# A graph network's first node stage: plain transposes, a split behind PSUM, and a longer pipeline

## What is computed

```python
# first layer (src, dst: edges; loops of weight 1 are added for every node)
deg = segment_sum(w_all, dst_all)
norm = deg**-0.5[src_all] * w_all * deg**-0.5[dst_all]
y = relu(segment_sum((x @ W)[src_all] * norm[:, None], dst_all) + b)
x1 = layernorm(x + y)
# second layer: per edge a filter from 20 radial numbers, scalar and vector
# products with the gathered x1[dst], a sum into x1's rows of src, two more
# matmuls, then out = layernorm(x1 + ...)
```

## Time and profile before

| what | us |
|---|---|
| median of 3 runs | 1240.66 |
| lowest and highest run | 1238.07, 1240.92 |
| the profiled execution | 1237.18 |
| its span | 1235.4 |
| PE busy in the span | 1004.6 (81%) |
| DVE, ACT, POOL busy | 840.1, 699.5, 657.0 |
| first and last start of L818 (nodes0) | 367.0, 664.1 |

### The profile page before, as it was taken

How to read it: one execution, slowest core, us unless ns; L and a number is a source line. 1 busy time by engine, 2 the same in 40 slices (tenths; PEclk the granted TensorE clock), 3 DMA queues, 4 the chain that set the end, 5 groups by cost and what they waited for, 6 DMA issues and landing times.

```text
span 1235.4 us, 23211 instructions
## 1 busy us (share of the span) xinstructions
PE 1004.6 (81%) x5088; PEld 788.5 (64%) x5088; DVE 840.1 (68%) x2538; ACT 699.5 (57%) x1632; POOL 657.0 (53%) x812
## 2 busy tenths in 40 slices
PE   6579998988749999999994788888888888834443
PEld 6557776776538888888883566666666666523332
DVE  7588777767327777777774566666566666448887
ACT  0168778867626666666663344343444434358887
POOL 2048888888547777777775455555555554310000
PEclk9999999989859999999998899999999999955555
DMA  9949999999976888888886678787777877579998
GB/s 359 419 147 242 242 253 231 248 236 237 214 177 212 271 283 277 282 279 279 278 276 213 178 176 182 170 171 178 168 173 176 183 168 155 77 204 348 349 350 296
DMA packets 175015, 289.00 MB, mean 234 GB/s; under 512 B 18514, under 2 KB 75750, under 8 KB 174966
## 3 DMA queue, kind: packets, MB, share of 16 engines
q1 hardware_dynamic: 120982, 176.23, 41.9%
q0 software_dynamic: 35840, 83.91, 36.0%
q10 hardware_dynamic: 18144, 28.32, 6.1%
HBM read 139.49 MB, written 148.90 MB: 233 GB/s over the span
## 4 chain that ended last, share of the span: by engine, by line
PE 28%; issue 18%; POOL 11%; DMA 5%; DVE 4%; ACT 4%; POOLq 2%; SPq 2%; DVEq 0%; ACTq 0%
PE bank L1079 6%; PE bank L1090 4%; PE bank L1100 4%; POOL tiny L463 3%; DMA node_mem<-sum 3%; PE bank L1088 3%; PE bank L1102 3%; PE bank L1103 3%; POOL tiny L466 3%; PE bank L1072 2%; PE bank L1086 1%; PE bank L1080 1%; POOL G_lo L476 1%; POOL tiny L470 1%; POOL tiny L468 1%
## 5 line engine op out<-in xcount | busy, mean ns | idle before, releaser
L500 POOL DMA_INDIRECT sum<-R_mem,l_sidx x80 | 127.9, 1599 | 173.7 <-ACT R_mem L636 167.4
L449 POOL DMA_INDIRECT sum<-R_mem,sidx_all x80 | 131.1, 1639 | 51.1 <-issue 29.3
L1052 PE MATMUL bank<-W0h,G_hi 128*128 128x512 f32 x320 | 134.0, 419 | 0.9 <-ACT G_lo L600 0.9
L1052 PE MATMUL bank<-W0h,G_lo 128*128 128x512 f32 x320 | 126.6, 396 | 0.0
L1052 PE MATMUL bank<-W0l,G_hi 128*128 128x512 f32 x320 | 126.3, 395 | 0.0
L611 ACT ACTIVATE node_mem<-node_mem,tiny 128x512 f32<-128x512 f32 x80 | 65.4, 817 | 91.2 <-POOL tiny L472 91.2
L476 POOL TENSOR_TENSOR G_lo<-node_mem,G_hi 128x512 fp32r<-128x512 f32 x80 | 104.1, 1301 | 19.4 <-ACT G_hi L607 19.4
L875 DVE SCALAR_TENSOR_TENSOR edge_mem<-edge_mem,Y,bank 128x128 f32<-128x128 f32 x240 | 73.1, 388 | 57.2 <-ACT edge_mem L630 42.5
L630 ACT COPY edge_mem<-bank 128x256 f32<-128x256 f32 x80 | 29.8, 372 | 135.8 <-PE bank L1090 135.8
L979 PE MATMUL bank<-G_hi,M_mem 128*128 128x512 f32 x200 | 88.4, 442 | 17.3 <-ACT R_mem L544 15.7
L492 POOL DMA_INDIRECT G_mem<-x_d,dst_i x80 | 79.5, 993 | 35.4 <-issue 16.2
(11 more groups left out here) (172 smaller groups left out, 2995.7 us busy)
## 6 DMA issues: line engine op xcount, KB each, us to landing
sum<-zeros ACTq DMA_DIRECT2D x42, 512.0 KB
filt_d<-node_mem SPq DMA_DIRECT2D x40, 512.0 KB
node_mem<-sum SPq DMA_DIRECT2D x80, 256.0 KB, 2.7
G_mem<-x SPq DMA_DIRECT2D x80, 256.0 KB, 2.8
x_d<-node_mem SPq DMA_DIRECT2D x80, 256.0 KB, 2.1
node_mem<-filt_d SPq DMA_DIRECT2D x80, 256.0 KB
sum<-node_mem SPq DMA_DIRECT2D x80, 192.0 KB, 2.3
out<-G_mem SPq DMA_DIRECT2D x20, 512.0 KB, 4.2
```

The costliest lines, as they stand in the source:

```text
L449: pool.indirect_dma_start(sum0, bass.IndirectOffsetOnAxis(ap=sidx[:, t:t + 1], axis=0), R[t % 8][:, :], None, compute_op=ALU.add).then_inc ...
L500: pool.indirect_dma_start(sum1, bass.IndirectOffsetOnAxis(ap=l1_sidx[:, t:t + 1], axis=0), R3[t % 8][:, :], None, compute_op=ALU.add).then ...
L1052: ins = pe.matmul(bank[4 + a][:, :], zt[b][:, c * P:(c + 1) * P], w[:, c, :], start=(c == 0 and k == 0), stop=(c == 3 and k == 2))
```

## The change

In nodes0:
- The identity of type f32r goes. PE transposes z itself (f32, four plain transposes), in step t + 1, into one of four banks.
- The split moves behind PSUM: ACT copies the bank to zT_hi (f32r) in step t + 2, DVE subtracts zT_hi from the bank into zT_lo in the same step. Each has four buffers. z_hi and z_lo, with ACT's L607, POOL's L476 and ACT's L600, go.
- PE runs the eight products with zT_hi first, then waits for zT_lo and runs the other four.
- DVE's max and sum (L827) go: ACT does Relu in place, POOL adds x, both in step t + 4. bn_stats and bn_aggr come two steps after that, in step t + 6. DVE's bank * dis + b stands last in its step.
- Ln, Exp and the root are done for two tiles at once, in every second step, on ACT and POOL; the root has seven instructions instead of five for one tile. The normalisation comes in step t + 9.
- res has eight buffers instead of four. SP stores in step t + 12, and its loads of sl wait for the transposes, its loads of xl for POOL's sum.
- Lead and tail of the loops grow (DVE, ACT and POOL: lead 16, tail 6 or 9; SP: lead 16, tail 12).

In edges0 the twelve gather semaphores become three, one for each group of four, and ACT waits once per group.

```diff
 @@ SP nodes0
-                    held(sp_, n_hi, s - 3)
-                    held(sp_, n_lo, s - 3)
+                    held(sp_, n_tr, s - 3)
                     sp_.dma_start(sl[a], rows(sum0, s)).then_inc(n_sl[a], 16)
-                    held(sp_, n_res, K_RES * (s - 7))
+                    held(sp_, n_sum, s - 7)
                     sp_.dma_start(xl[u], rows(x, s)).then_inc(n_xl[u], 16)
-                if live(s, 8):
-                    t = s - 8
+                if live(s, 12):
+                    t, a = s - 12, (u - 12) % 8
                     held(sp_, n_x1, t + 1)
...
 @@ POOL nodes0
+                if live(s, 7) and u % 2 == 0:
+                    t, a = s - 8, u // 2
+                    w, mean, var = tiny[a], mv[a][:, :, 0], mv[a][:, :, 1]
+                    st = Stage(n_rstd, g, K_ROOT)
+                    held(pool, n_mv, t + 2)
+                    st.mark(pool.tensor_scalar(w[:, 0, :], var, EPS, None, ALU.add))
+                    st.mark(pool.tensor_scalar(w[:, 7, :], mean, -1.0, None, ALU.mult))
+                    held(pool, n_rs, 2 * (g + 1))
+                    st.mark(pool.tensor_tensor(w[:, 3, :], w[:, 2, :], w[:, 2, :], ALU.mult))
+                    st.settle(pool)
+                    st.mark(pool.tensor_tensor(w[:, 4, :], w[:, 3, :], w[:, 0, :], ALU.mult))
                     held(pool, n_rstd, st.reached())
+                    st.mark(pool.tensor_scalar(w[:, 3, :], w[:, 4, :], -0.5, 1.5, ALU.mult, ALU.add))
                     st.settle(pool)
+                    st.mark(pool.tensor_tensor(w[:, 5, :], w[:, 3, :], w[:, 2, :], ALU.mult))
+                    st.settle(pool)
+                    st.mark(pool.tensor_tensor(w[:, 6, :], w[:, 7, :], w[:, 5, :], ALU.mult))
-                if live(s, 0):
-                    pool.wait_ge(n_hi, s + 1)
-                    wait(pool, n_tr, s - 3)
-                    pool.tensor_tensor(z_lo[u][:, :], sl[u], z_hi[u][:, :].bitcast(F32), ALU.subtract).then_inc(n_lo, 1)
+                if live(s, 4):
+                    t, a = s - 4, (u - 4) % 8
+                    pool.wait_ge(n_rel, t + 1)
+                    pool.tensor_tensor(res[a], res[a], xl[a], ALU.add).then_inc(n_sum, 1)
...
 @@ ACT edges0
+                    act.wait_ge(e_gather[(s - 1) % (NG // 4)], 64 * ((s - 1) // (NG // 4) + 1))
                     for q in (3, 2, 1, 0):
                         t = 4 * (s - 1) + q
-                        act.wait_ge(e_gather[t % NG], 16 * (t // NG + 1))
...
 @@ ACT nodes0, new order of a step
+                if tail:
+                    act.wait_ge(n_mv, t + 2)
+                    act.activation(tiny[a][:, 1, :], mv[a][:, :, 1], ACT.Ln, bias=eps_c[:, :]).then_inc(n_rs, 1)
                 if live(s, 2):
+                    t2, b = s - 2, (u - 2) % 4
+                    act.wait_ge(n_tr, t2 + 1)
+                    wait(act, n_mm, t2 - 3)
+                    act.copy(zT_hi[b][:, :], bank[b][:, :]).then_inc(n_hi, 1)
                     act.dma_start(sum1[bass.ds(t2 * P, P), 0:C], zeros[:, 0:C]).then_inc(s_zero1, 16)
+                if tail:
+                    act.wait_ge(n_rs, 2 * g + 1)
+                    act.activation(tiny[a][:, 2, :], tiny[a][:, 1, :], ACT.Exp, scale=-0.5).then_inc(n_rs, 1)
+                if live(s, 4):
+                    act.wait_ge(n_pre, t4 + 1)
+                    act.activation(res[c], res[c], ACT.Relu).then_inc(n_rel, 1)
+                if live(s, 9):
+                    act.wait_ge(n_rstd, K_ROOT * (g8 + 1))
+                    act.activation(res[c], res[c], ACT.Identity, bias=tiny[b][:, 6, k:k + 1], scale=tiny[b][:, 5, k:k + 1]) \
                        .then_inc(n_x1, 1)
...
 @@ DVE nodes0, new order of a step (z of step s, unchanged, stands first)
+                if live(s, 6):
+                    dve.wait_ge(n_sum, t + 1)
+                    dve.bn_stats(stat[c][:, :], res[a]).then_inc(n_bn, 1)
+                if live(s, 2):
+                    t, b = s - 2, (u - 2) % 4
+                    dve.wait_ge(n_hi, t + 1)
+                    wait(dve, n_mm, t - 3)
+                    dve.tensor_tensor(zT_lo[b][:, :], bank[b][:, :], zT_hi[b][:, :].bitcast(F32), ALU.subtract).then_inc(n_lo, 1)
+                if live(s, 6):
+                    if k == 0:
+                        held(dve, n_x1, t - 6)
+                    held(dve, n_bn, t + 1)
+                    dve.bn_aggr(mv[b][:, k, :], stat[a % 4][:, :]).then_inc(n_mv, 1)
                 if live(s, 4):
+                    dve.wait_ge(n_mm, t + 1)
+                    wait(dve, n_st[a], 32 * turn(t, a, 8))
+                    dve.scalar_tensor_tensor(res[a], bank[4 + c][:, :], dis[:, bass.ds(t, 1)], b0_s[:, :],
+                                             ALU.mult, ALU.add).then_inc(n_pre, 1)
...
 @@ PE nodes0
+                if live(s, 1):
+                    pe.wait_ge(n_z, t + 1)
+                    wait(pe, n_lo, t - 3)
+                    for c in range(4):
+                        ins = pe.transpose(bank[a][:, c * P:(c + 1) * P], sl[a][:, c * P:(c + 1) * P], ident[:, :])
+                    ins.then_inc(n_tr, 1)
                 if live(s, 3):
                     pe.wait_ge(n_hi, t + 1)
+                    wait(pe, n_pre, t - 3)
                     for c in range(4):
+                        for w in (W0h, W0l):
+                            pe.matmul(bank[4 + a][:, :], zT_hi[a][:, c * P:(c + 1) * P], w[:, c, :],
+                                      start=(c == 0 and w is W0h), stop=False)
+                    pe.wait_ge(n_lo, t + 1)
+                    for c in range(4):
+                        ins = pe.matmul(bank[4 + a][:, :], zT_lo[a][:, c * P:(c + 1) * P], W0h[:, c, :],
+                                        start=False, stop=(c == 3))
                     ins.then_inc(n_mm, 1)
```

More of the change, by code:

```diff
@@ L186, in build @@
         G_hi, G_lo = (ring(name, 8, [P, D], F32R) for name in ("G_hi", "G_lo"))
-        z_hi, z_lo = G_hi[:4], G_lo[:4]
+        zT_hi, zT_lo = G_hi[:4], G_lo[:4]
         NG = 12
@@ L190, in build @@
         junk1 = [b[:, 3 * D:3 * D + 256] for b in node_mem]
-        sl, res, W0_s = ([b[:, q * D:(q + 1) * D] for b in node_mem] for q in range(3))
+        sl, W0_s = ([b[:, q * D:(q + 1) * D] for b in node_mem] for q in (0, 2))
+        res = [b[:, q * D:(q + 1) * D] for q in (1, 2) for b in node_mem]
         xl = G
-        zT_hi, zT_lo = G_hi[4:6], G_lo[4:6]
         stat = ring("stat", 4, [P, 6])
-        mv = ring("mv", 4, [P, 2])
-        tiny = ring("tiny", 4, [P, 8])
+        mv = ring("mv", 4, [P, 2, 2])
+        tiny = ring("tiny", 4, [P, 8, 2])
         wst = [b[:, 0:1024].rearrange("p (v d) -> p v d", v=2) for b in node_mem]
@@ L247, in build @@
         e_lo = sem("e_lo")
-        e_gather = [sem(f"e_gather{i}") for i in range(NG)]
+        e_gather = [sem(f"e_gather{i}") for i in range(NG // 4)]
         e_M = sem("e_M")
@@ L267, in build @@
         n_x1 = sem("n_x1")
-        n_st = [sem(f"n_st{i}") for i in range(4)]
+        n_st = [sem(f"n_st{i}") for i in range(8)]
         f_trow = [sem(f"f_trow{i}") for i in range(4)]
@@ L586, in nodes0 @@
             def nodes0(s, u):
-                if live(s, 5):
-                    t, a = s - 5, (u - 5) % 4
-                    act.wait_ge(n_res, K_RES * (t + 1))
-                    act.activation(tiny[a][:, 1:2], mv[a][:, 1:2], ACT.Ln, bias=eps_c[:, :]).then_inc(n_rs, 1)
-                if live(s, 2):
-                    b, t2 = u % 2, s - 2
-                    act.wait_ge(n_tr, s - 1)
-                    wait(act, n_mm, s - 3)
-                    act.copy(zT_hi[b][:, :], bank[b][:, :]).then_inc(n_zT, 1)
@@ L608, in nodes0 @@
[L608 to L611 removed]
+                tail = live(s, 7) and u % 2 == 0
+                if tail:
+                    t, a = s - 8, u // 2
+                    g = t // 2 if isinstance(t, int) else (t - u) // 2 + a
+                    act.wait_ge(n_mv, t + 2)
+                    act.activation(tiny[a][:, 1, :], mv[a][:, :, 1], ACT.Ln, bias=eps_c[:, :]).then_inc(n_rs, 1)
@@ L1044, in nodes0 @@
                     ins.then_inc(n_tr, 1)
                 if live(s, 3):
-                    t, a, b = s - 3, (u - 3) % 4, (u - 3) % 2
-                    pe.wait_ge(n_zT, 2 * (t + 1))
-                    wait(pe, n_res, K_RES * (t - 3))
+                    t, a = s - 3, (u - 3) % 4
+                    pe.wait_ge(n_hi, t + 1)
+                    wait(pe, n_pre, t - 3)
                     for c in range(4):
-                        for k, (zt, w) in enumerate(((zT_hi, W0h), (zT_hi, W0l), (zT_lo, W0h))):
-                            ins = pe.matmul(bank[4 + a][:, :], zt[b][:, c * P:(c + 1) * P], w[:, c, :],
-                                            start=(c == 0 and k == 0), stop=(c == 3 and k == 2))
+                        for w in (W0h, W0l):
+                            pe.matmul(bank[4 + a][:, :], zT_hi[a][:, c * P:(c + 1) * P], w[:, c, :],
```

(1 more changed line is left out.)

94 lines of the change are left out of this document (27 added, 67 removed).

## The result

The changed kernel takes 1207.3 us (median of 4 runs, 1205.0 to 1213.0), the kernel before 1240.3 us: ratio 0.9744, 95% interval 0.9708 to 0.9780. That is 33 us less by the medians. The profiled executions took 1207.2 and 1237.2 us, so 30.0 us less, where the sum of the prediction gave 14.4 less.

The account below looks back on a forecast made before the run. The prediction took POOL's chain, 3.76 us per tile, as the bound, replaced by a 3.51 us DVE-ACT loop. With 1 us of head and 17.1 of drain the stage lost 14.4 us: 1224.5 us forecast, range 1206 to 1242.

Parts of the forecast that it names:

- the release to DVE: Loop term from the end of ACT's zT_hi to the begin of DVE's zT_lo: 0.14 us, read at L630 and L875.
- the drain: End of nodes0 after tile 77: POOL does three sums and three roots in a row, 17.1 us with normalisations.
- the head: Start of nodes0: with fewer transposes the clock may rise later, so the stage's first steps come 1 us later.
- POOL's own chain: Nodes0 in the kernel before: POOL's instructions set 3.76 us per tile, with PE 0.1 us behind.
- The loop that takes over: One-step loop in nodes0, DVE's bank x dis + bias, ACT's Relu to zT_hi, DVE's zT_lo and bn_aggr: 3.51 us.
- the lower end: Low end of the DVE-ACT loop: 3.36 us if releases cost 0.03 each and Relu is as short as the copy.
- two anchors: Whole kernel: 1222.8 us from the profiled execution and 1226.3 from the median of runs; 1224.5 taken between.
- the parts that I costed at nothing: Loads stay hidden, SP's longer lag lies under this, merged gather semaphores and dropping ident_r count for nothing.
- The weighed rule: Next DVE operation waits until the pipe is empty: loop 3.68 us, about 1238 us; part of the no-change rival, chance 0.11.
- The clock: Rival: PE idles 0.34 us per step, clock falls to 1.2 GHz, stage over 200 us longer; chance 0.02.
- PE as the bound: Rival in nodes0: loop terms overlap more than read, PE's 3.17 us per tile bounds, about 1198 us; chance 0.12.
- The slow case: Rival: Relu and neighbours run end to end, loop 3.96 us, about 1259 us, decides from 3.70; chance 0.15 including clock.

Follow-up runs that it names:

- experiment 6: Kernel before with only Ln, Exp and root done for two tiles at once, eight res buffers, later normalisation and stores; 1230.7 us, ratio 0.9913.
- experiment 1: Changed kernel with the normalisation placed ahead of Relu in ACT's step; 1196.0 us, ratio 0.9646.
- experiment 3: Changed kernel with bank x dis + bias moved to the front of DVE's step, ahead of z; 1196.4 us, ratio 0.9639.
- experiment 4: Changed kernel with one more ACT instruction per tile, a Relu of a constant tile, right behind Relu; 1246.1 us, ratio 1.0052.
- experiment 5: Changed kernel with one more ACT instruction per tile, a Relu of a constant tile, ahead of the wait before Relu; 1209.0 us, ratio 0.9745.
- experiment 8: Changed kernel with the DMA of zeros issued by SP instead of ACT; 1210.9 us, ratio 0.9750.
- experiment 9: Changed kernel with SP's stores in step t + 11 instead of t + 12; 1212.3 us, ratio 0.9786.
- experiment 10: Changed kernel with SP's stores in step t + 10 instead of t + 12; 1292.4 us, ratio 1.0428.
- experiment 7: Changed kernel with max and sum again one DVE instruction, one step behind bank x dis + bias, without ACT's Relu and POOL's sum; 1194.0 us, ratio 0.9614.
- experiment 2: Changed kernel with bank x dis + bias moved right behind z, ahead of bn_stats and zT_lo, on DVE; 1208.7 us, ratio 0.9740.

## Why the prediction was right or wrong

In short: the mechanism was right, a loop of one step between DVE and ACT; the sum was wrong in size. It gave 14.4 us less, and the stage became 31.5 us shorter. The terms that were mis-sized are the release to DVE above all, then the drain and the head.

**What bounds the kernel before: right.** POOL's own chain at 3.76 us and PE 0.1 us behind: experiment 6 lightened POOL and got PE's 3.65. The reading missed one thing in that chain: L463 took 0.53 us there because DVE was reading SBUF at that time (see the last section), and 0.21 us alone. Without that, POOL would have needed some 3.4 us (an estimate: 3.76 less 0.32) and not been the bound.

**The loop that takes over: right in kind, too long by 0.13 us per tile.** Both its waits appear in nearly every tile, and experiments 1, 3, 4 and 5 show that it bounds. The forecast had 3.51 us. The step between the L840 of tile 0 (364.60) and of tile 77 (624.77) is 3.38 us, 10.1 us less over 77 tiles. The terms:
- the release to DVE was the step that failed most: 0.14 from the earlier trace rows, measured 0.03 (at the median of 73 releases of L828; none is above 0.04). That is 0.11 x 77 = 8.5 of the 10.1 us. In the earlier trace rows the waiting instruction L875 takes its scalar at an address that depends on the tile, `Y[:, bass.ds(t, 1), i]`, which in the hardware loop comes from a register; zT_lo has no such operand, and it too runs in a hardware loop. The trace of the kernel before separates the two: in the steps written straight the same release takes 0.03 to 0.04 us (13 times), in the hardware loop 0.14 to 0.15 us (47 times). One from a straight step, ending at 693.95 and beginning at 693.99:

```profile
693.58 0.37 ACT L630 COPY edge_mem<-bank 128x256 f32<-128x256 f32 x1 [2.63 <-PE bank L1090]
...
693.99 0.91 DVE L875 SCALAR_TENSOR_TENSOR edge_mem<-edge_mem,Y,bank 128x128 f32<-128x128 f32 x3 [0.59 <-ACT edge_mem L630]
```

- bank x dis + bias 0.72 for 0.75, normalisation 0.71 for 0.73, Relu 0.54 for 0.52, the others within 0.01 of what was read.

I had the lower end at 3.36 and named its condition, releases of 0.03 each and a shorter Relu. (The terms named for the two ends add up to 3.34 and 3.95, not 3.36 and 3.96, and a ring of 3.70 lies at 1239 by the midpoint used, not at 1242; the forecast itself does not hang on these.) What I should have asked is whether a release of DVE had been measured on an instruction like the new one; the row I took was merely the nearest by engine pair.

**The drain: 17.1 us forecast, 13.5 measured** (L840 of tile 77 at 624.77, end at 638.3). The roots take 2.3 us for two tiles in the steady step, not 3.3, and 1.9, 1.9 and 2.8 us in the drain:

```profile
458.06 0.22 POOL L465 TENSOR_SCALAR tiny<-mv 128x2 f32<-128x2 f32 x1
...
459.47 0.70 POOL L474 TENSOR_TENSOR tiny<-tiny 128x2 f32<-128x2 f32 x1
460.25 0.20 POOL L476 TENSOR_TENSOR tiny<-tiny 128x2 f32<-128x2 f32 x1
460.40 1.29 POOL L480 TENSOR_TENSOR node_mem<-node_mem,G_mem 128x512 f32<-128x512 f32 x1
```

From 458.06 to 460.40 there are 2.34 us for seven instructions. I had scaled the old 2.36 us of five with the number of instructions, though the first of those five was long only in company: 0.53 us in the steady step of the earlier trace rows, 0.21 in the drain of the same trace, when DVE had less to do. Here it takes 0.22. POOL so needs (2 x 1.39 + 2.34) / 2 = 2.56 us per tile, where I had 3.0.

**The head: 1 us later forecast, 2.4 us earlier measured.** L840 of tile 0 began at 364.6, a miss of 3.4 us. Part of it is scatter between executions: the first z begins at 354.4 here and anywhere from 352.4 to 357.6 in the six other kernels with the same first steps (experiments 1, 4, 5, 8, 9, 10). The time from the first z to the first bank x dis + bias is steadier: 11.8 us in the kernel before (355.2 to 367.0) and 11.2 in experiment 6, which has the old first steps, but 9.2 to 10.3 us in those seven. So the head became 0.9 to 2.6 us shorter, where the prediction had it 1 us longer. PE's first transposes no longer wait for z_hi (they begin 0.9 us after the first z, before 1.55 us), and the granted clock reached 1.00 at about 364 us, before at 367 us; how much each is worth no run separates.

Together 10.1 + 3.6 + 3.4 = 17.1 us, which is the difference between -14.4 and the -31.5 of the stage. The forecast of 1224.5 lies 16.2 us under the median of 1240.7, where the sum gives 14.4: taking the middle of two anchors added 1.8 us in the right direction, which was luck. Of the parts that I costed at nothing, no load is waited for from 380 to 600 us, at a DMA share of 0.94, and the stores' longer lag shows in no wait there. The merged gather semaphores show in nothing that stands out of the scatter of the first z, and no run tests them alone.

**The weighed rule.** From the Trainium skill, page VectorE: DVE Perf Modes, section "The DRAIN you can't avoid", the prediction took a loop of 3.68 us, with which the change would have been worth nothing. The same section says that a next operation that is not held starts earlier, so the rule was quoted without its exception. In DVE's step above the begins lie 0.60 us apart after an instruction of 0.69 (454.52 and 455.12): the rows decide, and they decided rightly.

**The clock** stayed at 1.00 from 380 to 620 us, and also in experiment 10 from 380 to 590 us, with PE busy 158 of 210 us. One sign of being right did not come, PE busy some 90%: its records hide the short waits, as said above.

**The rivals.** PE as the bound was not what happened, but it lies only 0.18 us under the loop (3.20 us, where I had 3.17), and experiments 1, 3 and 7 reach it. The slow case needed a loop of 3.70 us; experiment 4 built one of 3.81 and came out 6 us above the kernel before.

## What to carry to other kernels

In a pipeline written as one program order per engine, look for closed ways of one step: follow each instruction to what it releases and to what stands behind it in the queue, and add begin-to-begin times. Such a loop costs time while every engine in it is idle a fifth or more, and moving one instruction in the order of either engine opens it (experiments 1 and 3), if it does not then meet another one at the wrong time (experiment 2). Before moving work to an idle engine, price the new round trip: here a version that left max and sum on DVE, one step behind, was as fast as any. And when a small term is borrowed from another place, a release between two engines for instance, look whether the instruction there is of the same kind.

## What the runs showed that was not expected

A DVE instruction with two inputs in SBUF (z, 0.74 us) became 1.39 us long at the median, up to 1.74, when POOL's 1.29 us sum ran at its beginning, and nothing in the waits tells of it; a change of order on DVE alone decides whether they meet (experiments 2 and 3). Its end can be forecast: 0.55 us behind the end of the POOL instruction. The kernel before had the same stall, smaller: 54 of its 59 z from 380 to 600 us begin during L476, and all 54 end 0.54 to 0.61 us behind it; z's own stall cost nothing there, since DVE was not the bound. POOL's small instructions show the other side: L474, 0.20 us in the drain, took 0.70 at 459.47 above, while z ran on DVE, and in all 33 cases from 380 to 600 us 0.64 to 0.71. In the kernel before, 55 of 59 L463 began beside z or L827 and took 0.52 to 0.75 us; the other four took 0.21. The DVE instruction of the case above:

```profile
459.38 0.74 DVE L819 SCALAR_TENSOR_TENSOR node_mem<-G_mem,dis,node_mem 128x512 f32<-128x512 f32 x1
```
